# Second layer of the experts with the weights as the stationary side, its output turned back by transpositions

## The reference

```python
scores = softmax(einsum('bsd,ed->bse', x, router_w), axis=-1)      # x: 1 x 2048 x 256, 8 experts
gate_vals, sel_idx = top_k(swapaxes(scores, 1, 2), capacity)       # capacity 513 for each expert
tokens = x[b_idx, sel_idx]
h = gelu(einsum('becd,edh->bech', tokens, w1) + b1)                # 256 -> 1024
y = einsum('bech,ehd->becd', h, w2) + b2                           # 1024 -> 256
out = zeros_like(x).at[b_idx, sel_idx].add(y * gate_vals[..., None])
```

## Time and profile before

| | |
|---|---|
| median of 3 runs | 1592.76 us (1590.61 to 1595.8) |
| the profiled execution, its own time | 1600.55 us |
| its span in the trace | 1598.8 us |
| busy in the span: PE / DVE / ACT / POOL | 1438.8 / 1012.5 / 663.0 / 976.7 us |
| mean granted clock of TensorE | 0.947 of full speed |

### The profile page before, as it was taken

One profiled execution on the slowest core, in us unless ns is written; L12 is line 12 of the kernel. 1 busy time (PEld: TensorE's weight loads), 2 busy tenths in 40 slices (PEclk: granted clock), 3 DMA queues, 4 the chain that ended last, 5 costly groups with the idle time before them and its releaser, 6 DMA issues. The chain is left out here.

```text
span 1598.8 us, 25447 instructions
## 1 busy us (share of the span) xinstructions
PE 1438.8 (90%) x9169; PEld 915.0 (57%) x9169; DVE 1012.5 (63%) x1639; ACT 663.0 (41%) x800; POOL 976.7 (61%) x448
## 2 busy tenths in 40 slices
PE   4989999999999999999999999999968616999992
PEld 4655555555555555555455555554448606999992
DVE  7556676676666767667666666767426474756740
ACT  3224444444444444444444444444532104455460
POOL 2126776677676667767667766787864022667673
PEclk8989999999999999999999999999978757999996
DMA  7430011001001000100100110011134241444321
GB/s 225 175 106 1 21 37 33 14 15 55 15 21 51 14 15 21 56 14 14 51 14 21 34 36 14 15 47 45 36 130 171 95 139 29 119 105 95 82 40 17
DMA packets 87853, 89.50 MB, mean 56 GB/s; under 512 B 22953, under 2 KB 68026, under 8 KB 87626
## 3 DMA queue, kind: packets, MB, share of 16 engines
q1 hardware_dynamic: 68657, 79.16, 15.1%
q0 software_dynamic: 19072, 8.70, 3.7%
HBM read 59.49 MB, written 27.99 MB: 55 GB/s over the span
## 5 line engine op out<-in xcount | busy, mean ns | idle before, releaser
L687 POOL TENSOR_TENSOR acc_p<-acc_p,x_in 128x1024 f32<-128x1024 f32 x224 | 567.9, 2535 | 248.5 <-ACT x_in L751 242.5
L92 DVE TENSOR_REDUCE mx_part<-ps_m 128x1 f32<-128x512 f32 x744 | 478.9, 685 | 320.5 <-PE ps_m L80 318.2
L751 ACT ACTIVATE x_in<-ps_s 128x1024 f32<-128x1024 f32 x384 | 377.8, 1024 | 323.2 <-PE ps_s L603 318.5
L615 PE MATMUL ps_o<-x_in,v 128*64 128x512 f32 x1664 | 406.2, 606 | 0.0
L615 PEld LDWEIGHTS ps_o<-x_in,v 128*64 128x64 f32 x1664 | 99.5, 136 | 178.3 <-issue 141.8
L598 PE MATMUL ps_s<-q,k 64*128 64x512 f32 x1248 | 183.9, 394 | 0.0
L603 PE MATMUL ps_s<-m_rows,ones_row 64*128 64x512 f32 x832 | 173.4, 392 | 0.0
L598 PEld LDWEIGHTS ps_s<-q,k 64*128 64x128 f32 x1248 | 123.1, 187 | 20.5
L687 POOL TENSOR_TENSOR acc_p<-x_in 128x1024 f32<-128x1024 f32 x32 | 76.0, 2375 | 65.6 <-ACT x_in L751 64.7
L623 POOL TENSOR_TENSOR acc_p<-acc_p,acc_d 128x1024 f32<-128x1024 f32 x32 | 76.7, 2396 | 57.8 <-DVE acc_d L687 57.6
L80 PE MATMUL ps_m<-k_hi,q_hi 64*128 64x512 f32 x384 | 102.7, 460 | 7.8 <-issue 2.9
(11 more groups left out here) (246 smaller groups left out, 2362.0 us busy)
## 6 DMA issues: line engine op xcount, KB each, us to landing
w_in<-in_w SPq DMA_DIRECT2D x16, 1024.0 KB, 8.5
v_st<-rec_scr SPq DMA_DIRECT2D x64, 128.0 KB, 2.9
o_scr<-v_st SPq DMA_DIRECT2D x32, 256.0 KB, 2.1
v_scr<-c_in SPq DMA_DIRECT2D x13, 512.0 KB, 2.6
v<-v_scr SPq DMA_DIRECT2D x8, 832.0 KB, 5.2
ot<-o_scr SPq DMA_DIRECT2D x2, 2048.0 KB, 11.4
x_in<-in_x SPq DMA_DIRECT2D x4, 512.0 KB, 7.6
x<-in_x SPq DMA_DIRECT2D x4, 512.0 KB, 10.3
```

Of the source, the lines that this page charges most:

```text
L92: dve.tensor_reduce(part[:, j // S.MF, j % S.MF:j % S.MF + 1], bank[:, 0:S.MC], AX.X, ALU.max).then_inc(G.rough_used[hd], 1)
L615: last = pe.matmul(ps_o[hd * HP:hd * HP + DH, :], v[b][:, s, hd * DH:(hd + 1) * DH], probs[:, g % RING, hd * QC:(hd + 1) * QC], start=(s = ...
L687: eng.tensor_tensor(acc, other, probs[:, (u * KT + t) % RING, :], ALU.add).then_inc(done, 1)
L751: act.activation(probs[:, g % RING, :], ps_s[:, g % 2, :], ACT.Exp, bias=G.pad_bias[:, 0:1] if s == KT - 1 else 0.0, scale=SCALE).then_inc ...
```

## The change

The second layer changes sides. w2 is stationary and the tokens are moving, as in the first layer: 4 products (2 halves of the tokens x 2 blocks of 128 features) of 24 matmuls with 258 columns. Two of the four results lie in banks of `ps_h` (so the first layer's blocks use the banks in the other order). The result lies as feature x token; b2 is now one value for each partition, and ACT adds it as it copies the result to SBUF (`yt`, `act_y`). PE then turns it back, 2 transpositions for each of the 5 token tiles (`pe_turn`), and DVE multiplies by the gate (`dve_y`). Tiles 2, 3 and 4 are turned in the next expert, after its blocks 1, 2 and 3. Two small copies on DVE keep the gates and b2 of an expert (`dve_gate`), so that the gather no longer waits for the last `y`. b2 is loaded once in 16 rows and turned instead of spread.

The orders change too. PE makes the list of e+1 ahead of block 0 instead of after it. ACT does `w2_hi` right after `w1_hi`. DVE does `w1_lo` and `dve_hot` right after the last `h_lo`, ahead of the `xgt_lo`, the gate's copies and the first `y`.

```diff
-        b2_sb = sb("b2_sb", [RT, E, D])
+        b2_in, b2_t = sb("b2_in", [E * KD, P]), sb("b2_t", [P, E, KD])
+        b2_e = [sb(f"b2_e{b}", [P, KD]) for b in range(2)]
...
+        gate = [sb(f"gate{b}", [RT, ST]) for b in range(2)]
+        yt = sb("yt", [P, KD, NS])
...
+            if h == 1:
+                wait_for(pe, yt_done, YB * e)
...
-        def pe_y(pe, e, b, j):
-            if j == 0:
+        def y_bank(n):
+            c, k = divmod(n, KD)
+            return (ps_y[:, c, 0:HS], ps_h[:, 0, c, 0:HS])[k], k, slice(c * HS, (c + 1) * HS)
+        def pe_y(pe, e, b, n):
+            out, k, cols = y_bank(n)
+            if n == 0:
                 pe.wait_ge(w2_lo_done, e + 1)
-            wait_for(pe, y_done, ST * e + j - 1)
-            m = rows[j] + rows[j] % 2
-            bank = (ST * b + j) % 2
+                wait_for(pe, y_done, ST * e - 1)
+            elif n == 1:
+                pe.wait_ge(gelu_done, HT * (e + 1))
+            elif n == 2:
+                wait_for(pe, y_done, ST * e)
             for h in range(HT):
-                if j == 0:
+                if n == 0:
                     pe.wait_ge(h_lo_done, HT * e + h + 1)
-                for n, (x, w) in enumerate(((h_hi, w2_hi[b]), (h_hi, w2_lo[b]), (h_lo, w2_hi[b]))):
-                    last = pe.matmul(ps_y[0:m, bank, 0:D], x[:, h, j * RT:j * RT + m], w[:, h, :],
-                                     start=(h == 0 and n == 0), stop=(h == HT - 1 and n == 2))
+                for m, (w, x) in enumerate(((w2_hi[b], h_hi), (w2_lo[b], h_hi), (w2_hi[b], h_lo))):
+                    last = pe.matmul(out, w[:, h, k * P:(k + 1) * P], x[:, h, cols], start=(h == 0 and m == 0),
+                                     stop=(h == HT - 1 and m == 2))
             last.then_inc(y_ready, 1)
-        def dve_y(dve, e, i, b, j):
+        def act_y(act, e, b, n):
+            src, k, cols = y_bank(n)
+            act.wait_ge(y_ready, YB * e + n + 1)
+            wait_for(act, yt_turned, ST * e)
+            act.wait_ge(b2_moved, e + 1)
+            act.activation(yt[:, k, cols], src, ACT.Identity, bias=b2_e[b][:, k:k + 1]).then_inc(yt_done, 1)
+        def turned_bank(j):
+            return ps_y[0:rows[j], (0, 0, 1, 0, 1)[j], 0:D]
+        def pe_turn(pe, e, j):
+            pe.wait_ge(yt_done, YB * e + (2 if j < 2 else YB))
+            if j != 0 and j != 2:
+                pe.wait_ge(y_done, ST * e + (0, 1, 0, 2, 3)[j])
+            for k in range(KD):
+                last = pe.transpose(turned_bank(j)[:, k * P:(k + 1) * P], yt[:, k, j * RT:j * RT + rows[j]], G.ident[:])
+            last.then_inc(yt_turned, 1)
+        def dve_gate(dve, e, i, b):
+            dve.wait_ge(gathered[b], 16 * ST * (i + 1))
+            wait_for(dve, y_done, ST * (e - 1))
+            wait_for(dve, yt_done, YB * (e - 1))
+            dve.tensor_copy(b2_e[b][:], b2_t[:, at(e), :].rearrange("p o k -> p (o k)")).then_inc(b2_moved, 1)
+            dve.tensor_copy(gate[b][:], xg[b][:, :, at(D + e)].rearrange("p j o -> p (j o)")).then_inc(gate_kept, 1)
+        def dve_ids(dve, e, i, b):
+            wait_for(dve, scattered[b], 16 * ST * i)
+            dve.tensor_copy(idx_s[b][:], idx_g[b][:]).then_inc(idx_kept, 1)
+        def dve_y(dve, e, b, j):
             n = rows[j]
-            dve.wait_ge(y_ready, ST * e + j + 1)
-            if j == 0:
-                wait_for(dve, scattered[b], 16 * ST * i)
-                dve.tensor_copy(idx_s[b][:], idx_g[b][:]).then_inc(idx_kept, 1)
-            y = ps_y[0:n, (ST * b + j) % 2, 0:D]
-            dve.tensor_tensor(y, y, b2_sb[0:n, at(e), :].rearrange("p o d -> p (o d)"), ALU.add).then_inc(y_biased, 1)
-            dve.wait_ge(y_biased, ST * e + j + 1)
-            dve.tensor_scalar(y_sb[b][0:n, j, :], y, xg[b][0:n, j, at(D + e)], None, ALU.mult).then_inc(y_done, 1)
+            dve.wait_ge(yt_turned, ST * e + j + 1)
+            dve.tensor_scalar(y_sb[b][0:n, j, :], turned_bank(j), gate[b][0:n, j:j + 1], None, ALU.mult).then_inc(y_done, 1)
...
         def pe_expert(pe, e, i, b, last):
+            first = isinstance(e, int) and e == 0
+            if not last:
+                pe_list(pe, e + 1, 1 - b)
             for h in range(HT):
                 pe_h(pe, e, b, h)
-                if h == 0 and not last:
-                    pe_list(pe, e + 1, 1 - b)
-            for j in range(ST):
-                pe_y(pe, e, b, j)
-                if not last:
-                    for n in {0: (0, 1), 1: (2,)}.get(j, ()):
-                        pe_xgt(pe, e + 1, *nxt(i, b), n)
+                if 1 <= h <= 3 and not first:
+                    pe_turn(pe, e - 1, h + 1)
+            for n in range(YB):
+                if n == YB - 1 and not last:
+                    pe_xgt(pe, e + 1, *nxt(i, b), 2)
+                pe_y(pe, e, b, n)
+                if n == 1 and not last:
+                    for m in range(2):
+                        pe_xgt(pe, e + 1, *nxt(i, b), m)
+                if n >= 2:
+                    pe_turn(pe, e, n - 2)
+            if last:
+                for j in range(2, ST):
+                    pe_turn(pe, e, j)
         def act_expert(act, e, i, b, last):
             for h in range(HT):
                 act_h(act, e, h)
             if not last:
                 act_w1_hi(act, e + 1, *nxt(i, b))
-                for n in range(TJ):
-                    act_xgt(act, e + 1, n)
                 act_w2_hi(act, e + 1, *nxt(i, b))
+            for n in range(YB):
+                act_y(act, e, b, n)
+                if not last:
+                    for m in {1: (0, 1), 2: (2,)}.get(n, ()):
+                        act_xgt(act, e + 1, m)
         def dve_expert(dve, e, i, b, last):
+            first = isinstance(e, int) and e == 0
             hot = not (isinstance(e, int) and e + 2 >= E)
             if not last:
                 dve_index(dve, e + 1, *nxt(i, b))
             for h in range(HT):
                 dve_h(dve, e, h)
-            for j in range(ST):
-                dve_y(dve, e, i, b, j)
-                if not last:
-                    for n in {0: (0, 1), 1: (2,)}.get(j, ()):
-                        dve_xgt(dve, e + 1, n)
-                    if j == 1:
-                        w1_lo_of(dve, e + 1, 1 - b)
-                if j == 2 and hot:
+                if 1 <= h <= 3 and not first:
+                    dve_y(dve, e - 1, 1 - b, h + 1)
+            dve_ids(dve, e, i, b)
+            if not last:
+                w1_lo_of(dve, e + 1, 1 - b)
+                if hot:
                     dve_hot(dve, e + 2, b)
+                for m in range(2):
+                    dve_xgt(dve, e + 1, m)
+                dve_gate(dve, e + 1, *nxt(i, b))
+            dve_y(dve, e, b, 0)
+            if not last:
+                dve_xgt(dve, e + 1, 2)
+            for j in range(1, ST if last else 2):
+                dve_y(dve, e, b, j)
...
+                sp.dma_start(b2_in[:], A["b2"].rearrange("e (k p) -> (e k) p", p=P)).then_inc(b2_loaded, 16)
                 sp_weights(sp, 0, 0, 0)
                 sp_weights(sp, 1, 0, 1)
-                sp.dma_start(b2_sb[:], A["b2"].rearrange("(o e) n -> o (e n)", o=1).to_broadcast([RT, E * D])
-                             .rearrange("p (e n) -> p e n", e=E)).then_inc(b2_loaded, 16)
```

More of the change, by code:

```diff
@@ L1209, in phase_experts @@
         w2_loaded = [sem(f"w2_loaded{b}") for b in range(2)]
-        b2_loaded = sem("b2_loaded")
+        b2_loaded, b2_turned, b2_kept, b2_moved = (sem(n) for n in ("b2_loaded", "b2_turned", "b2_kept", "b2_moved"))
         w1_hi_done, w1_lo_done, w2_hi_done, w2_lo_done = (sem(n) for n in ("w1_hi_done", "w1_lo_done", "w2_hi_done", "w2_lo_done"))
@@ L1215, in phase_experts @@
         h_ready, gelu_done, h_hi_done, h_lo_done = sem("h_ready"), sem("gelu_done"), sem("h_hi_done"), sem("h_lo_done")
-        y_ready, y_biased, y_done = sem("y2_ready"), sem("y2_biased"), sem("y2_done")
+        y_ready, yt_done, yt_turned, y_done, gate_kept = (sem(n) for n in ("y2_ready", "yt_done", "yt_turned", "y2_done", "gate_kept"))
         def sp_weights(sp, e, i, b):
@@ L1340, in pe_h @@
                 for n, (w, x, k) in enumerate(terms):
-                    last = pe.matmul(ps_h[:, h % 2, c, 0:HS], w[:, k, cols], x[:, k, c * HS:(c + 1) * HS],
+                    last = pe.matmul(ps_h[:, (h + 1) % 2, c, 0:HS], w[:, k, cols], x[:, k, c * HS:(c + 1) * HS],
                                      start=(n == 0), stop=(n == len(terms) - 1))
@@ L1347, in act_h @@
             wait_for(act, h_lo_done, HT * e + h - 1)
-            act.activation(h_f[:, h % 2, :].rearrange("p (c n) -> p c n", c=2), ps_h[:, h % 2, :, 0:HS], ACT.Gelu,
+            act.activation(h_f[:, h % 2, :].rearrange("p (c n) -> p c n", c=2), ps_h[:, (h + 1) % 2, :, 0:HS], ACT.Gelu,
                            bias=G.b1_t[:, b1_col(e, h)]).then_inc(gelu_done, 1)
@@ L1512, in _ @@
                 act_w2_hi(act, 0, 0, 0)
+                act.wait_ge(b2_turned, 1)
```

(3 more changed lines are left out.)

9 lines of the change are left out of this document (5 added, 4 removed).

## The result

The changed kernel takes 1624.1 us (median of 4 runs, 1623.2 to 1629.4) where the kernel before took 1592.0 on the same chip: a ratio of 1.0205, 95% interval 1.0176 to 1.0233. It is 32 us slower; 1598.5 was forecast.

A forecast was written before the change was run, and what follows sets the result against it. PE was taken as the bound, with DVE and POOL excluding each other and scatters setting the end. +0.5 + 0.2 + 3 x 2.0 - 0.9 = +5.8, say 5.7 us, on 1592.76 gave 1598.5; range 1579 to 1605.

The forecast's parts named there:

- The place and the chain of the loss: POOL's `w2_lo` holds DVE's `row_hot`, making `xgt_lo` late; PE stands 3.5 us and loses 1.1 us to clock per expert.
- The last term: End of program: expert 5's first scatter comes 9.15 us after expert 6's list, not 10.05 (-0.9); the 72.3 us behind stay.
- PE's own time: PE per expert: 24 matmuls fewer (-2.85 us), ten transpositions at 0.1 each (+1.0), so 27.84 becomes 26.0 us.
- the second of "what bounds the kernel now": DVE and POOL: a POOL subtraction and a two-SBUF-input DVE instruction exclude each other; `w2_lo` takes 4.49 us alone, the later starter waits.
- the first rival: `row_hot` starts at 19.4, ahead of POOL's 19.6: 26.7 us per expert, 1585.9 us, or 1577 with experts 1 and 2; chance 0.34.
- PE's wait: PE ahead of the third group of transpositions, reached at t = 23.0, needs the first `xgt_lo` at 26.5: stands 3.5 us.
- Something stalls there that the change doesn't touch: Experts 1 and 2 take 3.1 and 2.5 us more with the same 242 matmuls; forecast 31.75 each, +0.2 together.
- Up to the list of expert 2: Expert 0: no scatter, `hot` instructions wait for `w2_lo`, the list ahead fills a wait: about +0.5 us, -0.6 without clock loss.
- Worse: Stalls of experts 1 and 2 return in full and transpositions cost the skill page's figure: +10 to +16, 1603 to 1609; chance 0.08.
- No exclusion is felt: DVE and POOL don't hold each other, PE sets the time: 26.2 us per expert, -19, 1573.6 us; chance 0.07.

## Why the prediction was wrong

**The place and the chain of the loss were right.** DVE's `hot` operations are held by `w2_lo`, PE stands ahead of the third group for `xgt_lo`, and clock is lost behind it. The last term, the scatters that set the end, was 1.6 us off: from the list of expert 6 to expert 5's first scatter it is 8.84 us (forecast 9.15), but the 72.3 behind it became 74.3; 1.5 of that is the fifth scatter of that expert, stretched by `w1_lo` as well (5.42 us). The direction was right too.

**PE's own time was nearly right.** Forecast were 26.0 us of PE for an expert; without holds it is 26.1 to 26.2. A block with a pair of turns behind it takes 1.66 us instead of 1.44, so the pair costs 0.22 where 0.2 was taken. PE reached the third group at t = 22.7 (forecast 23.0). The 275 ns that the Trainium skill (TensorE: Matmul & The Clock Gate, Part 4) gives for a transposition is the length of its row here too (median 271 ns of the 50 in experts 1 to 5). But the next operation starts before it ends, so that one costs about 0.11 us in the stream.

**The step that failed is the second of "what bounds the kernel now": "the 1.4 more are the time in which DVE's `w1_lo` was still running".** From it came 4.49 us as the price of `w2_lo` and the time of its start as the start of the hold. But 1508.02 + 5.92 - 4.49 is 1509.45, and the fifth scatter of the earlier trace rows ends at 1505.41 + 3.90 = 1509.31: the 1.4 us were the wait for the scatter's end. In expert 5 before, the two ends (1509.16 and 1509.31) lie too close to decide it; the changed kernel does. There `w1_lo` ends at 1458.05 and the scatter at 1461.82, and `w2_lo` ends 4.53 behind the scatter. (In experts 1 and 2 before, where `w2_lo` comes behind the scatter's end, the extra length is indeed `w1_lo`'s: 1391.18 + 4.49 = 1395.67, and `w2_lo` ends at 1395.66.) What came of it, in expert 3 with t from the list at 1439.37:
- POOL's `w2_lo` was forecast from t = 19.6 to 24.1 and ran from 20.7 to 27.0. Of the 2.9 us, 1.75 are the row's length (6.24 instead of 4.49), 1.1 its later start. The fifth scatter now overlaps DVE's `w1_lo` and takes 5.42 us instead of 3.90. The forecast had left POOL's chain as it was, though it moved `w1_lo` ahead of the fifth scatter's start.
- DVE was forecast to be held from 19.9. It was held from 18.9, before the row of `w2_lo` begins. The 0.3 us by which POOL was to be first were no margin at all. DVE came 0.7 us sooner than forecast (`w1_lo` at t = 16.4, not 17.1), so that by the forecast's own rule `row_hot` would have started near 19.2, ahead of POOL's 19.6: the condition of the first rival, "faster", was met. The hold came all the same, since it begins beside the scatter.
- PE's wait: forecast 3.5 us, measured 6.92. That is 3.4 us too little in experts 3 to 5 and 3.1 in 1 and 2 (by their 30.15), 16 of the 18.3 us by which the forecast for experts 1 to 5 is short (24.5 against 6.2). The clock was priced somewhat low: PE is busy for 27.5 to 28.7 us where 26.15 do at full clock, 1.35 to 2.5 and 1.85 in the mean against the 1.1 taken.

**Experts 1 and 2.** "Something stalls there that the change doesn't touch" was wrong: the waits for `h_f` of the kernel before are absent from these experts in the changed kernel, and also when `dve_hot` alone moves. Their cause stays open. Because their stall was taken as given, they were forecast at 31.75 us each, +0.2 in all; they now take 34.9 and 34.6.

**Up to the list of expert 2** the forecast was +0.5 and the trace has +3.7, of which 1.3 lie ahead of the experts, where nothing was changed but b2's load. In expert 0, which has no scatter, `w2_lo` holds `tile_hot` 4.63 us, PE waits 3.27 us, and the fourth product ran wholly at the lower clock, 5.2 us instead of 2.85.

**The rivals.** None had the hold begin beside the scatter. "Worse" had a hold of another kind and 275 ns as the price of a transposition, and ended at 1609. "No exclusion is felt" (1573.6) is what one wait on POOL and `dve_hot` early make true: 1573.8. That the two numbers agree is luck, since the kernel before took 1601.5 on that chip: the gain is 28 us where the rival had 19. Its single condition was in reach of the program.
